# A mixture-of-experts layer on one core: the opening's loads on two queues, its first chunk in halves of the features

## The chip, the cores and the metric

One core of a Trainium2 chip runs the whole program. The metric is the device time of one execution, in microseconds; the number for the kernel before is the median of three executions.

## The reference

The input x has 128 rows of 64 tokens with 512 features (8192 tokens), and there is one condition vector of 256 numbers per row. All is float32. What is computed, in short:

```
q      = relu(cond @ W3 + b3)                       # one vector of 512 per row
h      = relu(((64 * x + sum of the row's 64 tokens) * q) @ W2 + b2)
scores = softmax(h @ gate_w.T); the 6 best of 64 experts per token
y      = for each token, its experts' SwiGLU (width 352), each weighted by its score;
         an expert takes its first 64 tokens
shared = (silu(h @ sw_gate) * (h @ sw_up)) @ sw_down      # width 704
out    = x + y + shared
```

The experts take their first 64 tokens in the order of the token numbers, so the first stage must have seen all tokens before the experts' gathers start.

## The kernel before, in words

The 8192 tokens are 16 chunks of 512 (CH). For each chunk the first stage makes h transposed (features on partitions) in four squares of 128 features; from h it makes the gate's logits, the routing, and, for every second chunk, the shared part. The second stage does the experts and the rest of the shared part. TensorE's matmuls mostly take float32r operands, a value being split into a high and a low part, three matmuls for one product (`three`, lines 1395 to 1398). The order of work on each engine is written out by hand; engines wait for each other by counting semaphores (`wait_ge`). `body(i)` does chunks 2i+1 and 2i+2.

What this case is about is the opening, up to the first `body`.

- **Loads.** SP issues nearly all: cond (line 471), W3 as one transfer of 512 KB (472), the first half of x's first chunk in four quarters (473; `load_x`, 396), W2 in four (479), the other half of the first chunk, the second chunk in four, the gate's weights (482), then the shared weights in pieces (`load_piece`). A quarter q of x or W2 goes to partitions 32q to 32q+31 only, since x is turned by VectorE in squares of 32 by 32. ACT issues the two biases, each as four loads of 128 elements one by one (`load_bias`, 724): b3 first of all, b2 behind its copy of W3.
- **q.** TensorE transposes cond (1529), ACT copies it (734), ACT and VectorE each reorder half of W3 (736, 1294), TensorE makes q with 16 matmul passes (1536), ACT takes it with bias and relu for all 128 rows into `qb` (743), each of 4 instructions for 128 features.
- **x's chain.** For each half chunk (8 blocks of 32 tokens, 128 partitions by 1024 elements) VectorE runs five operations, `x_turn`, `x_sum`, `x_pair`, `x_shift`, `x_scale` (874 to 907): the turn, the sum over each block's tokens, the sum of two blocks to a row of 64 tokens, 64 x + sum, and times q. Each waits for the one before by `x_step`.
- **W2.** ACT reorders W2 to `w2p` by columns, one copy for each block oc of 128 output features (749), each with all four blocks k of input features, then makes its high part (`split_piece(0)`).
- **First products.** `cond_half` (1417) multiplies the first chunk and the first half of the second with plain float32, two passes for a matmul (line 1429): for each half, for each oc, all four k. The second half of the second chunk goes by `three`. Then ACT takes h (`take_cond`), VectorE makes its low part (`split_h`), and `logits_raw` (1445) makes the gate's logits; for these VectorE first makes the low part of the gate's weights (1319). Which waits hold TensorE at `logits_raw(0)`: hh and hl of each square, and `gw2_ready` of both engines.
- **Fillers.** `keep_clock(n)` (1520) has TensorE transpose the identity n times into a bank that nobody reads, so that it is busy while it would wait: 6, 14 and 68 times.
- **VectorE's order** from line 1290: waits for the presets, POOL's iotas and W3; its half of W3; the first chunk's two halves; the second chunk's, mixed with the low parts of W2 and h; gate weights; rows of h (`take_rows`); `split_xm(1, 1)`, which in the kernel before also waits for `cond_begun`, since `w2p` lies where `xml1` is written.
- **POOL** makes the identity and two iotas (576 to 583) and then sleeps until the experts.

## Time and profile before

| | us |
|---|---|
| median of three executions | 1226.82 |
| lowest, highest | 1226.76, 1227.08 |
| the profiled execution, its own time | 1216.14 |
| its span, first to last instruction | 1214.4 |
| PE (TensorE matmul) busy | 1207.5 (99%) |
| PEld (weight load) busy | 893.5 (74%) |
| DVE (VectorE) busy | 856.1 (70%) |
| ACT (ScalarE) busy | 332.0 (27%) |
| POOL (GpSimd) busy | 271.0 (22%) |

A span's time is counted from the first instruction. "Busy" for PE includes matmuls that wait in its pipeline, so the spacing of weight loads (PEld) says more about its pace than the share. In the rows below, a line such as "8.78 1.25 DVE L880 ... [2.41 <-DMA x]" reads: started at 8.78, ran 1.25 us, on VectorE, line 880 of the kernel, and VectorE had been idle for 2.41 us before it, until the transfer named. SPq and ACTq are the issues of transfers on an engine's queue; their durations are those of the issue and not of the transfer. An "x4" merges four instructions, with the time from the first start to the last end.

### The profile page before, as it was taken

Reading aid. Unit: us, or ns where it says so; the run is one execution under the profiler, and the core shown is the slowest. Engines: PE = TensorE matmul, PEld = TensorE weight load, DVE = VectorE, ACT = ScalarE, POOL = GpSimd, SP = SyncE. Lnnn points to the kernel's source line nnn. Section 1 sums busy time; section 2 is a strip of 40 time slices with the busy share of each in tenths; the row PEclk is TensorE's granted clock in tenths of the full one; section 3 lists DMA queues with packets and bytes.
Section 4 is the critical chain, followed back from the end, with each engine's and each line's share of the span. In section 5 each row is a group of like instructions: output and inputs, shape, how many; then the busy total and the mean of one; then the engine's idle time right before and its main releaser. Section 6 shows DMA issues by size and latency. Waiting matters only on the chain.

```text
span 1214.4 us, 15974 instructions
## 1 busy us (share of the span) xinstructions
PE 1207.5 (99%) x5764; PEld 893.5 (74%) x5764; DVE 856.1 (70%) x1851; ACT 332.0 (27%) x630; POOL 271.0 (22%) x246
## 2 busy tenths in 40 slices
PE   9999999999999999999999999999999999999998
PEld 8888888888888888888866666666666666666666
DVE  6998989989889888886656555664655654655652
ACT  4544243433423443244111111110111201111111
POOL 0000000000000000000254356253453553543431
PEclk9999999999999999999999999999999999999999
DMA  9857445272643726246766988988979889889763
GB/s 199 212 137 194 97 118 134 83 174 64 164 106 86 183 74 157 57 134 194 248 242 232 333 278 276 346 270 273 333 249 340 291 287 295 299 290 307 275 149 86
DMA packets 159824, 250.92 MB, mean 207 GB/s; under 512 B 23617, under 2 KB 94401, under 8 KB 158593
## 3 DMA queue, kind: packets, MB, share of 16 engines
q1 hardware_dynamic: 143968, 223.66, 58.3%
q0 software_dynamic: 14048, 25.18, 10.2%
q10 hardware_dynamic: 1728, 1.05, 0.3%
q8 instruction: 46, 0.75, 0.3%
q14 instruction: 34, 0.27, 0.1%
HBM read 197.14 MB, written 61.10 MB: 213 GB/s over the span
## 4 chain that ended last, share of the span: by engine, by line
PE 94%; DVE 4%; issue 1%; ACT 0%; DMA 0%; SPq 0%; ACTq 0%
PE bank L1396 23%; PE bank L1397 22%; PE bank L1398 22%; PE bank L1598 12%; PE bank L1613 7%; PE bank L1429 2%; PE bank L1516 1%; PE bank L1517 1%; PE bank L1454 1%; PE bank L1452 1%; PE bank L1523 1%; PE bank L1465 1%; DVE x L880 0%; DVE prod L947 0%; DMA w3s<-in_L_cond_W_dram 0%
## 5 line engine op out<-in xcount | busy, mean ns | idle before, releaser
L1396 PE MATMUL bank<-hh,gu 128*128 128x512 f32 x704 | 278.0, 395 | 0.0
L1397 PE MATMUL bank<-hl,gu 128*128 128x512 f32 x704 | 274.2, 390 | 0.0
L1398 PE MATMUL bank<-hh,gu 128*128 128x512 f32 x704 | 274.0, 389 | 0.0
L591 POOL DMA_INDIRECT hg<-table,idx_quarter x128 | 125.2, 978 | 635.5 <-DVE idx_hi L1282 596.8
L1396 PEld LDWEIGHTS bank<-hh,gu 128*128 128x128 f32 x704 | 132.1, 188 | 39.1 <-issue 12.8
L1398 PEld LDWEIGHTS bank<-hh,gu 128*128 128x128 f32 x704 | 132.1, 188 | 27.9
L1397 PEld LDWEIGHTS bank<-hl,gu 128*128 128x128 f32 x704 | 132.2, 188 | 26.2
L651 ACT ACTIVATE ah<-prod 128x512 fp32r<-128x512 f32 x96 | 60.6, 632 | 302.3 <-DVE prod L947 302.3
L1355 DVE STREAM_TRANSPOSE eactT<-eact 32x96 f32<-32x96 f32 (+1 forms) x512 | 133.9, 261 | 7.9
L1396 PE MATMUL bank<-sdh,ah 128*128 128x512 f32 x320 | 125.9, 393 | 0.0
L1397 PE MATMUL bank<-sdl,ah 128*128 128x512 f32 x320 | 124.6, 389 | 0.0
L1398 PE MATMUL bank<-sdh,al 128*128 128x512 f32 x320 | 124.5, 389 | 0.0
L708 ACT ACTIVATE prod<-bank 128x512 f32<-128x512 f32 x96 | 57.1, 595 | 190.7 <-PE bank L1398 190.7
L947 DVE TENSOR_TENSOR prod<-bank,prod 128x512 f32<-128x512 f32 x96 | 65.6, 684 | 46.0 <-PE bank L1398 35.6
L1396 PE MATMUL bank<-xmh,w2h 128*128 128x512 f32 (+1 forms) x240 | 92.4, 385 | 0.0
L1398 PE MATMUL bank<-xmh,w2l 128*128 128x512 f32 (+1 forms) x240 | 91.8, 383 | 0.0
L1397 PE MATMUL bank<-xml,w2h 128*128 128x512 f32 (+1 forms) x240 | 91.7, 382 | 0.0
L1613 PE MATMUL bank<-wd,eactT 128*64 128x512 f32 (+1 forms) x384 | 89.5, 601 | 0.0
L1369 DVE TENSOR_SCALAR ysc<-bank,hsc 64x512 f32<-64x512 f32 x64 | 48.0, 750 | 56.7 <-PE bank L1613 52.6
L1343 DVE TENSOR_TENSOR eact<-bank,esilu 128x352 f32<-128x352 f32 x32 | 16.8, 525 | 99.9 <-PE bank L1598 99.9
L606 POOL DMA_INDIRECT out_dram<-ysc,idx_pair x32 | 47.8, 1494 | 157.9 <-DMA out_dram<-outst 96.8
L1598 PE MATMUL bank<-wg,hgt 128*64 128x352 f32 x512 | 81.2, 459 | 0.0
(125 smaller groups left out, 1709.9 us busy)
## 6 DMA issues: line engine op xcount, KB each, us to landing
wg<-in_L_ffn_w_gate_dram SPq DMA_DIRECT2D x64, 704.0 KB, 9.2
wu<-in_L_ffn_w_up_dram SPq DMA_DIRECT2D x64, 704.0 KB, 10.8
wd<-in_L_ffn_w_down_dram SPq DMA_DIRECT2D x64, 512.0 KB, 5.1
table<-hrow SPq DMA_DIRECT2D x64, 256.0 KB, 4.3
x<-in_x_dram SPq DMA_DIRECT2D x60, 256.0 KB, 7.0
wd<-in_L_ffn_w_down_dram SPq DMA_DIRECT2D x64, 192.0 KB, 6.1
out_dram<-outst SPq DMA_DIRECT2D x36, 256.0 KB, 4.6
outst<-in_x_dram SPq DMA_DIRECT2D x32, 256.0 KB, 3.4
```

Source lines behind the costliest of these rows:

```text
L591: nc.gpsimd.indirect_dma_start(out=hg[p % 3][:, b, :], out_offset=None, in_=quarters, in_offset=bass.IndirectOffsetOnAxis(ap=idx_quarter[: ...
L606: nc.gpsimd.indirect_dma_start(out=of, out_offset=bass.IndirectOffsetOnAxis(ap=idx, axis=0), in_=ysc[p % 3][e * CAP:(e + 1) * CAP, :], in_ ...
L651: return nc.scalar.activation(o, i, ACT.Copy)
L708: nc.scalar.activation(prod[0:m, i % 2, :], bank[t % 3][0:m, :], ACT.Silu).then_inc(s.silu_ready, 1)
L947: nc.vector.tensor_tensor(prod[0:m, i % 2, :], bank[t % 3][up0:up0 + m, :], prod[0:m, i % 2, :], ALU.mult).then_inc(s.prod_ready, 1)
L1355: op = nc.vector.transpose(eactT[feats, 0:n, tok], squares[:, 0:n, feats])
L1369: op = nc.vector.tensor_scalar(ysc[p % 3][rows, :], bank[6][rows, :], hsc[p % 3][rows, at:at + 1], None, ALU.mult)
L1396: nc.tensor.matmul(o, st_h, mv_h, start=first_mm, stop=False)
L1397: nc.tensor.matmul(o, st_h, mv_l, start=False, stop=False)
L1398: return nc.tensor.matmul(o, st_l, mv_h, start=False, stop=last_mm)
L1598: op = nc.tensor.matmul(o[half, 0:I], hgt[:, k, half], w[p % 2][e][:, k * I:(k + 1) * I], start=(k == 0), stop=(k == KC - 1))
L1613: op = nc.tensor.matmul(bank[6][half, :], eactT[0:m, it, half], wd[e][0:m, it, :], start=(it == 0), stop=(it == IT - 1))
```

## The change

Four things change, all ahead of the first `body`.

1. **Loads on two queues.** Quarters 0 and 1 (partitions 0 to 63) of x's first two chunks and of W2 stay on SP, quarters 2 and 3 (partitions 64 to 127) go to ACT's queue, between ACT's own work. W3 is one half on each. W2 comes in two steps, first the blocks k = 0, 1 of input features, then k = 2, 3.
2. **Biases as rows.** POOL loads both biases as rows of 32 elements into a cleared tile `brow`; VectorE turns it in four squares into `bcol`, where they are columns. `bias_ready` replaces the two bias waits of ACT. POOL does it ahead of its iotas, for which VectorE waits.
3. **q in two steps.** TensorE signals after each pair of 128-feature blocks; ACT takes at first only the rows that the first two chunks need (16 of 128), and the rest behind W2's copies.
4. **First chunk in halves of the features.** `x_begin` does one turn, and then sum, pair sum, shift and scale for features 0, 1 (of the four blocks k) and 2, 3 apart; `cond_first` multiplies k = 0, 1 for all four oc as soon as these are there (`x_early`), then k = 2, 3. W2 is reordered by k and not by oc. The fillers are 8, 5 and 12 in place of 6, 14 and 68.

`w2p` now lies in `xml`'s place, so `cond_begun` is gone, and SP waits for the first raw logits before it loads the fourth chunk.

```diff
@@ places and helpers
-        w2p = Place(xml1_at)("w2p", [P, KC, D])
+        w2p = Place(xml_at)("w2p", [P, KC, D])
+        bt = Place(eactT_at)
+        brow = bt("brow", [SQ, P])
+        bcol = bt("bcol", [P, SQ])
+        b3c, b2c = bcol[:, 0:KC], bcol[:, KC:2 * KC]
+        def q_of(fc):
+            return bank[3 + fc // 2][:, fc % 2 * B:(fc % 2 + 1) * B]
+        PAIRS = (slice(0, KC // 2), slice(KC // 2, KC))
+        def w2_rows(q, pair):
+            return rows_of(W2, q)[:, PAIRS[pair], :], w2s[q * SQ:(q + 1) * SQ, PAIRS[pair], :]
+        def x_quarter(n, q, half=None):
...
@@ SP
+                if n == 3:
+                    sp.wait_ge(s.lraw_filled, 1)
...
             sp.dma_start(conds[:, :], cond).then_inc(s.cond_loaded, 16)
-            sp.dma_start(w3s[:, :, :], W3.rearrange("(k p) o -> p k o", p=P)).then_inc(s.w3_loaded, 16)
-            load_x(0, 0)
+            sp.dma_start(w3s[:, 0, :], W3[0:P, :]).then_inc(s.w3_loaded, 16)
+            begin_x(0)
+            begin_w2(0)
+            begin_w2(1)
+            begin_x(1)
+            for q in range(2):
+                src, dst = x_quarter(1, q)
+                sp.dma_start(dst, src).then_inc(x_loaded[1], 16)
...
-            load_piece(0)
-            load_x(0, 1)
-            load_x(1)
@@ POOL
+            pool.wait_ge(s.bias_cleared, 1)
+            for r, b in enumerate((b3, b2)):
+                pool.dma_start(brow[r * KC:(r + 1) * KC, :].rearrange("k (q j) -> k q j", j=SQ),
+                               b.rearrange("(q k j) -> k q j", k=KC, j=SQ)).then_inc(s.bias_loaded, 16)
@@ ACT
-            load_bias(b3, b3c)
+            act.dma_start(w3s[:, 1, :], W3[P:2 * P, :]).then_inc(s.w3_loaded, 16)
...
+            begin_x(0)
             act.wait_ge(s.presets, 1)
             silu_table()
             act.wait_ge(s.condT_filled, 1)
             copy(condT[:, :, :], bank[5][:, 0:QC * B].rearrange("p (k b) -> p k b", k=QC)).then_inc(s.condT_ready, 1)
-            act.wait_ge(s.w3_loaded, 16)
+            begin_w2(0)
+            begin_w2(1)
+            act.wait_ge(s.w3_loaded, 32)
             copy(w3p[:, 1, :]...).then_inc(s.w3_ready, 1)
-            load_bias(b2, b2c)
...
+            act.wait_ge(s.bias_ready, 1)
+            for pair in range(2):
+                act.wait_ge(s.q_filled, pair + 1)
+                for fc in range(2 * pair, 2 * pair + 2):
+                    op = take_q(fc, 0, 2 * CH // N)
+                op.then_inc(s.q_ready, 1)
+            begin_x(1)
+            for q in range(2, P // SQ):
+                src, dst = x_quarter(1, q)
+                act.dma_start(dst, src).then_inc(x_loaded[1], 16)
+            def order_w2(k):
+                copy(w2p[:, k, :].rearrange("p (o a j) -> p o a j", o=KC, j=SQ),
+                     w2s[:, k, :].rearrange("p (a o j) -> p o a j", o=KC, j=SQ)).then_inc(s.w2_ready, 1)
+            act.wait_ge(s.w2_begun, 16 * (P // SQ))
+            order_w2(0)
+            order_w2(1)
+            act.wait_ge(piece_loaded[0], 16 * len(pieces[0][0]))
+            order_w2(2)
+            order_w2(3)
+            split_piece(0)
+            for fc in range(KC):
+                op = take_q(fc, 2 * CH // N, B)
             op.then_inc(s.q_ready, 1)
...
@@ VectorE
+            def x_begin(half):
...
+                x_turn(0, half)
+                total(0, 1)
+                both_halves(0, 2)
+                shift(0, 3)
+                total(1, 1)
+                scale(0, 4)
+                both_halves(1, 5)
+                shift(1, 6)
+                scale(1, 7)
...
-                    dve.wait_ge(s.cond_begun, 1)
...
+            nc.vector.memset(brow[:, :], 0.0).then_inc(s.bias_cleared, 1)
...
-            x_half(0, 0)
-            x_turn(0, 1)
-            x_sum(0, 1)
-            x_pair(0, 1)
-            x_shift(0, 1)
-            x_scale(0, 1)
+            dve.wait_ge(s.bias_loaded, 32)
+            for q in range(P // SQ):
+                part = slice(q * SQ, (q + 1) * SQ)
+                op = nc.vector.transpose(bcol[part, :], brow[:, part])
+            op.then_inc(s.bias_ready, 1)
+            x_begin(0)
+            x_begin(1)
@@ TensorE
+            def full(n, oc, half, k):
+                t = slice(half * (CH // 2), (half + 1) * (CH // 2))
+                return nc.tensor.matmul(cond_bank(n, oc)[:, t], w2p[:, k, oc * P:(oc + 1) * P], half_of(n, half)[:, :, k, :],
+                                        start=(k == 0), stop=(k == KC - 1))
+            def cond_first(half):
+                pe.wait_ge(s.x_early, half + 1)
+                for k in range(KC // 2):
+                    pe.wait_ge(s.w2_ready, k + 1)
+                    for oc in range(KC):
+                        full(0, oc, half, k)
+                pe.wait_ge(s.xm_ready, half + 1)
+                pe.wait_ge(s.w2_ready, KC)
+                for oc in range(KC):
+                    for k in range(KC // 2, KC):
+                        op = full(0, oc, half, k)
+                    if half == 1:
+                        op.then_inc(s.cond_filled, 1)
...
-            keep_clock(6)
+            keep_clock(8)
...
-            keep_clock(14)
+            keep_clock(5)
...
-            op.then_inc(s.q_filled, 1)
-            keep_clock(68)
-            for half in range(2):
-                for oc in range(KC):
-                    cond_half(0, oc, half)
+                if fc % 2 == 1:
+                    op.then_inc(s.q_filled, 1)
+            keep_clock(12)
+            cond_first(0)
+            cond_first(1)
```

## Rows read from the trace of the kernel before

**Rows 1.** Waits of PEld over the whole span: total us, times, longest.
```profile
PEld bank L1598 <- issue: 85.9, 510, 0.3
...
PEld bank L1516 <- DVE ah L865: 1.9, 1, 1.9
...
PEld bank L1454 <- DVE hl L865: 1.1, 2, 0.6
```
**Rows 2.** Chain of waits, 0 to 80 us: start, duration, what.
```profile
6.62 2.02 PE bank L1536 x16
8.64 7.42 PE bank L1523 x68
16.07 13.81 PE bank L1429 x64
```
**Rows 3.** Timeline of the opening, VectorE: start, duration, instruction, idle before it.
```profile
8.78 1.25 DVE L880 STREAM_TRANSPOSE x<-x 128x1024 f32<-128x1024 f32 x1 [2.41 <-DMA x<-in_x_dram]
...
15.90 1.25 DVE L880 STREAM_TRANSPOSE x<-x 128x1024 f32<-128x1024 f32 x1 [1.88 <-DMA x<-in_x_dram]
...
19.91 1.22 DVE L906 TENSOR_TENSOR x<-x,qb 128x1024 f32<-128x1024 f32 x1
...
21.80 1.25 DVE L880 STREAM_TRANSPOSE x<-x 128x1024 f32<-128x1024 f32 x1 [0.66 <-DMA x<-in_x_dram]
...
36.40 0.42 DVE L865 TENSOR_TENSOR gw<-bank,gw 128x256 fp32r<-128x256 f32 x1
```
**Rows 4.** Timeline, TensorE: the first matmul of the raw logits.
```profile
37.02 0.58 PE L1452 MATMUL bank<-hh,gw 128*128 128x512 f32 x1
```
**Rows 5.** Timeline from 43 to 96 us, weight loads and VectorE.
```profile
47.14 0.19 PEld L1454 LDWEIGHTS bank<-hl,gw 128*128 128x128 f32 x1 [0.54 <-DVE hl L865]
...
49.25 3.04 DVE L865 TENSOR_TENSOR gu<-gu_in,gu 128x1024 fp32r<-128x1024 f32 x3 [0.69 <-ACT gu L651]
...
94.29 0.68 DVE L865 TENSOR_TENSOR hl<-h,hh 128x512 fp32r<-128x512 f32 x1
...
95.03 0.19 PEld L1454 LDWEIGHTS bank<-hl,gw 128*128 128x128 f32 x1 [0.59 <-DVE hl L865]
```
**Rows 6.** Groups by line and shape, VectorE: busy us, mean ns; one by min/median/max ns.
```profile
L897 DVE SCALAR_TENSOR_TENSOR x<-x,vsum 128x1024 f32<-128x1024 f32 x4 | 4.9, 1223 | 0.1
...
L865 DVE TENSOR_TENSOR hl<-h,hh 128x512 fp32r<-128x512 f32 x4 | 2.7, 684 | 0.0
...
L1355 DVE STREAM_TRANSPOSE eactT<-eact x512: 237/268/274, 614.0 to 1183.2; 32x96 f32<-32x96 f32 x128, 32x64 f32<-32x64 f32 x43
```
**Rows 7.** Windows of the opening: busy PE, PEld, DVE, ACT, POOL, clock, DMA share, GB/s.
```profile
2.00:3.00 1.00, 1.00 (x6) 0.67 (x4) 0.00 (x0) 0.32 (x1) 0.00 (x0) 1.00 0.66 144
3.00:5.00 2.00, 1.98 (x10) 1.91 (x10) 0.00 (x0) 1.44 (x3) 0.00 (x0) 1.00 0.98 315
5.00:7.00 2.00, 1.75 (x12) 1.54 (x11) 0.43 (x1) 0.63 (x1) 0.00 (x0) 1.00 1.20 234
9.00:20.00 11.00, 11.00 (x84) 10.52 (x83) 8.85 (x10) 6.22 (x12) 0.00 (x0) 1.00 1.20 209
```
**Rows 8.** Window of a wide load (sw_down, 128 partitions).
```profile
51.00:52.00 1.00, 1.00 (x6) 0.84 (x5) 1.00 (x2) 0.45 (x1) 0.00 (x0) 1.00 1.15 347
```
**Rows 9.** Timeline of the opening: issues of ACT, fillers, smallest memset, copies of ACT.
```profile
0.75 1.90 ACTq L727 DMA_DIRECT2D b3c<-in_L_cond_b_dram  x4
...
1.54 0.07 DVE L1289 MEMSET zx<- 128x8 f32 x1
...
3.58 2.79 PE L1523 MATMUL bank<-ident 128*128 128x128 f32 x14
...
5.84 0.63 ACT L651 ACTIVATE w3p<-w3s 128x512 f32<-128x512 f32 x1 [1.40 <-DMA w3s<-in_L_cond_W_dram]
...
13.22 2.19 ACT L651 ACTIVATE w2p<-w2s 128x512 f32<-128x512 f32 x4 [2.26 <-DMA w2s<-in_L_cond_W_dram]
```
**Rows 10.** POOL's transfers: one in the timeline, and their us from issue to landing.
```profile
601.33 0.95 POOL L591 DMA_INDIRECT hg<-table,idx_quarter  x1 [0.30 <-issue]
...
DMA to landing us min/median/max: 2.4/5.5/8.1
```

More of the change, by code:

```diff
@@ L269, in adaln_moe_ffn_kernel @@
         piece_loaded = [sem(f"piece_loaded{n}") for n in range(1 + GT // 2 + 1 + 2)]
-        bias_loaded = [sem(f"bias_loaded{n}") for n in range(2)]
         x_begun = [sem(f"x_begun{h}") for h in range(2)]
@@ L293, in rows_of @@
             return w[q * P:(q + 1) * P, :].rearrange("(k j) i -> j k i", j=SQ)
-        pieces = [([(rows_of(W2, q), w2s[q * SQ:(q + 1) * SQ, :, :]) for q in range(P // SQ)],
+        def q_of(fc):
[4 more added lines that the diff above has]
+        def x_quarter(n, q, half=None):
+            b = slice(0, NB) if half is None else slice(half * (NB // 2), (half + 1) * (NB // 2))
+            rows = xf[n * CH + b.start * SQ:n * CH + b.stop * SQ, :].rearrange("(b i) d -> i b d", i=SQ)
+            return rows[:, :, q * P:(q + 1) * P], x32[q * SQ:(q + 1) * SQ, n % 2, b, :]
+        pieces = [([w2_rows(q, 1) for q in range(P // SQ)],
                    [(w2h[:, :, oc * P:(oc + 1) * P].rearrange("p k (a j) -> p k a j", j=SQ),
@@ L722, in split_piece, with begin_x, begin_w2 @@
                     copy(h_part, src).then_inc(s.piece_split_h, 1)
-            def load_bias(b, c):
-                with nc.allow_non_contiguous_dma(reason="a vector of 512 elements, once"):
-                    for q in range(P // SQ):
-                        act.dma_start(c[q * SQ:(q + 1) * SQ, :],
-                                      b[q * P:(q + 1) * P].rearrange("(k j) -> j k", j=SQ)).then_inc(bias_loaded[c is b2c], 16)
-            load_bias(b3, b3c)
+            act.dma_start(w3s[:, 1, :], W3[P:2 * P, :]).then_inc(s.w3_loaded, 16)
+            def begin_x(half):
+                for q in range(2, P // SQ):
+                    src, dst = x_quarter(0, q, half)
+                    act.dma_start(dst, src).then_inc(x_begun[half], 16)
+            def begin_w2(pair):
+                for q in range(2, P // SQ):
+                    src, dst = w2_rows(q, pair)
+                    act.dma_start(dst, src).then_inc(piece_loaded[0] if pair else s.w2_begun, 16)
+            begin_x(0)
             act.wait_ge(s.presets, 1)
@@ new lines, in _ @@
+            begin_x(1)
+            for q in range(2, P // SQ):
+                src, dst = x_quarter(1, q)
[7 more added lines that the diff above has]
+            act.wait_ge(piece_loaded[0], 16 * len(pieces[0][0]))
@@ L875, in x_turn @@
                 if n == 0:
-                    dve.wait_ge(x_begun[half], 64)
+                    dve.wait_ge(x_begun[half], 16 * (P // SQ))
                 elif half == 0:
@@ L1422, in cond_half @@
                     wait(pe, s.cond_taken, oc - 1)
-                if n == 0 or half == 0:
-                    pe.wait_ge(s.w2_ready, oc + 1)
+                if half == 0:
+                    pe.wait_ge(s.q_ready, 3)
                     pe.wait_ge(s.xm_ready, 2 * n + half + 1)
-                    x = half_of(n, half)
                     for k in range(KC):
-                        op = nc.tensor.matmul(cond_bank(n, oc)[:, t], w2p[:, k, oc * P:(oc + 1) * P], x[:, :, k, :],
-                                              start=(k == 0), stop=(k == KC - 1))
+                        op = full(n, oc, half, k)
                 else:
@@ L1441, in cond_half @@
                     op.then_inc(s.cond_filled, 1)
-                elif n == 1 and oc == KC - 1:
-                    op.then_inc(s.cond_begun, 1)
             def logits_raw(n):
@@ L1535, in _ @@
                 for k in range(QC):
[L1536 removed]
+                    op = nc.tensor.matmul(q_of(fc), w3p[:, k, fc * P:(fc + 1) * P],
                                           condT[:, k, :], start=(k == 0), stop=(k == QC - 1))
[L1538 to L1542 removed]
+                if fc % 2 == 1:
[3 more added lines that the diff above has]
+            cond_first(1)
             pe.wait_ge(s.gate_ready, 1)
```

90 lines of the change are left out of this document (61 added, 29 removed).

## The prediction

> **What bounds the kernel now.** I read the list of waits first. Over the whole span the longest waits of TensorE's weight loads for another engine are 1.9 and 1.1 us; the rest is "issue" between back-to-back matmuls [rows 1]. So TensorE is the bound, and the time falls only by what lets its dense work start earlier. The chain of waits shows where it is not dense: the load of W3, 16 matmuls of q, then 68 filler transposes (7.42 us) that compute nothing, and only at 16.07 the first useful product [rows 2]. The fillers stand for a wait, and VectorE's timeline says for what: its first transpose of x begins at 8.78, when x has landed; the half chunk takes it 5.23 us, to 14.01, and TensorE can't multiply before that.
>
> The reader is to see next that the first product is not what decides. VectorE works without a hole from 21.80, when the second chunk lands, to 36.82, the end of the gate's low part (36.40 plus 0.42) [rows 3]. The matmul that needs it, the first of the gate's raw logits, starts at 37.02 [rows 4]. So from 21.80 on TensorE follows VectorE with 0.2 us between them. After that everything hangs together: TensorE waits 0.54 us for hl at 47.14, VectorE 0.69 us for a piece at 49.25 and is then dense until the hl of 94.29, for which TensorE waits 0.59 us at 95.03 [rows 5]. No such wait comes later. Whatever 37.02 moves by, 95.03 and the end move by too: the links between are waits, not transfers (SP's issues up to there only come earlier). I call this move G: how much earlier VectorE ends its gate part, if TensorE can follow.
>
> **The change, part by part.**
>
> *VectorE's work.* One half chunk is now 5.23 us (15.90 to 21.13) [rows 3]. x_begin cuts sum, pair-add, shift and scale into halves of the features: nine instructions for five. A 512-element operation took 0.68 against 1.22 for 1024 [rows 6]; a dependent one starts 0.03 behind the end before, an independent one 0.1 ahead of it. Starts: turn 0, sum 1.28, pair 2.0, shift 2.2, second sum 2.8, scale 3.4, pair 4.0, shift 4.2, scale 4.9, next turn 5.55. The first pair of squares is out at 4.1, all at 5.6. From start to next start that is 5.55 against 5.13, so the cut costs VectorE 0.8 us in all (0.4 if the small ones overlap better, 1.2 if each waits). The 15.02 us behind (21.80 to 36.82) are unchanged.
>
> *Transfers.* x's first half, W3 and cond are 1.18 MB. They moved at 144 GB/s from 2 to 3, at 315 to 5 and 234 to 7, and had landed by 8.78, some 1.5 us behind their last bytes. From 9 to 20, where each transfer fills 32 partitions, the rate is 209 [rows 7]; wide transfers reach 347 on the same engines later [rows 8]. So the narrow shape, not the engines, limits. Now SP issues partitions 0 to 63 and ACT 64 to 127, both at once. No row has two such streams; the bounds are 209 and 347. I take 310, near the 315 of 3 to 5, where x's quarters began beside the wide W3. Then 1.18 MB need one microsecond at 288 and 2.9 at 310: 5.9, landed at 7.4.
>
> The Trainium skill speaks against this. "DMA: Bandwidth & Descriptors", section "Rules for kernel authors", says that spreading transfers over queues saves issue time only, and that two transfers to disjoint partition halves serialize. "SBUF — State Buffer", section "Door 1: The DMA port swizzle", says that partitions 0 to 63 reach only 8 of 16 ports (about 218 GB/s) and 64 to 127 the other 8, by which the split used here is the one that could double the rate; 209 in rows 7 agrees with its figure for 8 ports. By the first rule G is that of rival 2.
>
> *Biases.* Eight tiny loads leave ACT's queue (1.90 us to issue four [rows 9]); two go to POOL, behind one memset of VectorE (0.07). POOL's DMA instructions took 0.95 with 0.30 between them and landed 2.4 to 8.1 after issue [rows 10]: issued at 1.5 and 2.75, they land between 5.2 and 10.9; I take 6.3, nearer the first, since these carry 2 KB each. The iotas behind them end near 4.4, ahead of W3. VectorE copies w3p (0.43) and turns four 32x32 squares, each between 0.07 (its smallest memset [rows 9]) and 0.27 (32x96 [rows 6]), say 1.0 in all. So VectorE starts on x at 7.5: x allows 7.4, the biases 7.3.
>
> *ACT, TensorE's clock and q.* condT stays bound by TensorE's transposes (copied at 4.1). Then come four issues of W2 at 0.47, to 6.1, in front of w3p's copy (0.63 [rows 9]): q's 16 matmuls start at 6.9, not 6.62. The fillers' pace shows the clock: 14 in 2.79 us, 0.20 each (the 1.2 GHz level) up to 6.4, and 68 in 7.42, 0.11 each (2.4 GHz), behind q [rows 2, 9]. Now only 8, 2 and 5 precede a pause from 4.6 to 6.9, so the clock may rise later. q takes 2.0 if it is high, 16 x 0.21 = 3.4 if low; I take 3.0, low at first and rising within q: 9.9. With takes of 0.25 each (32 columns: between 0.07, the smallest operation, and the 0.63 of a copy of 512) q is ready at 10.5, in time for the first scale at 10.9. But four x issues stand behind it on ACT (to 12.4), and in front of w2p's copies (2.19 for four [rows 9]): 12.9, 13.5, 14.0, 14.6. ACT has few transfers in flight, so I expect no stall like SP's 3.06 us. The second half's ACT quarters, issued 10.5 to 11.4, land about 2.5 later, at 13.9; VectorE is free at 13.05 and waits 0.85. The second chunk lands by 18, ahead of need.
>
> *TensorE's product.* It starts at 13.0 (w2p; the early squares are there at 11.6) and takes 13.81 for 64 matmuls [rows 2]; the second half's early squares are out at 13.9 + 4.1 = 18.0, ahead of need at 19.9. It ends at 26.8 against 29.88; gate transposes 0.39, second chunk's first half 7.1: 34.3. The waits for the rest of q (ACT, near 20) and for gate_ready are hidden by the product. Moving w2p to xml's place and dropping the wait for cond_begun cost nothing: xml is first written past 62. SP's new wait for the raw logits ends 1 us after its old one, with some 15 us before that load is issued.
>
> *Sum.* VectorE starts the second chunk at 13.9 + 5.55 = 19.45 in place of 21.80: **G = 2.35**. Its gate part ends at 34.5, the logits start at 34.65, TensorE is ready at 34.3. The 3.1 us that the product gains are thus cut by VectorE.
>
> The profiled execution took 1216.14 with a span of 1214.4, so 1.7 lies around the span; the median of the runs is 1226.82, 10.7 more. G lies inside the span and is taken from the median: 1226.82 - 2.4 = 1224.4.
>
> **Rivals.**
> 1. *The clock is high by the start of q.* For it: fillers run from 1.54 to 4.6. Against: the pause. q ends at 8.9, ACT's steps come 1.0 to 1.2 earlier, x's second half no longer waits: VectorE 7.5 + 5.55 + 5.55 = 18.6, G = 3.2, TensorE ready at 33.3 and the logits at 33.8: 1223.6.
> 2. *No more bandwidth from two queues.* x at 8.2 (the first microsecond is fuller), the second half's 2.75 MB near 15.6 as at 15.90 now: VectorE 15.6 + 5.55 = 21.15, G = 0.65: 1226.2. For it: nothing in the rows shows two streams that add up; against: that wide ones reach 347 on the same engines.
> 3. *The pause behind q costs the clock.* 12 fillers end near 11.3, the product starts at 13.0. If the clock falls for as long as it took to rise (1.54 to about 6), TensorE loses up to 2 us of product and G is 0.4 to 1.2: 1226.0.
> 4. *Slower: the biases come late.* VectorE's whole chain stands behind bias_loaded. It decides from a landing at 6.5 on and loses a us per us once past x's; slower than before from 9.7 on (start 10.7, second chunk at 21.8). At the worst row, 10.9, the second chunk starts at 23.0: G = -1.2, 1228.0; a first use of POOL's queue may cost more.
> 5. *Nothing*: the fillers are only shorter, and other waits take the gain: 1226.8.
>
> **How the numbers follow.** Forecast 0.37, rival 1 0.21, rival 2 0.22, rival 3 0.06, rival 4 0.07, rival 5 0.07. A measurement of this kernel can tell about 0.2%, 2.45 us, from no change. The forecast sits on that line and gives half its 0.37 to faster, rival 1 nearly all: 0.38. Slower by more needs biases past 12: 0.04. The rest, 0.58, lies within. Predicted 1224.4. The range goes from 1222.9 (rival 1 with a cut that costs VectorE less; TensorE caps it at 3.7) to 1226.9 (rivals 2 and 5). The forecast's own range is 1223.7 to 1225.2.
>
> **What would show it.** x's first turn at 7.5 (6.8 to 8.2); a rate near 310 from 4 to 9; 64-column scales at 0.68; q's matmuls 0.21 apart, then 0.11; the first product near 13, the second chunk's turn near 19.5; a short wait in front of the raw logits; the waits near 45 and 92.7 unchanged in size. Wrong if the first turn starts after 8.5, if VectorE idles over 1.5 us before the second half, or if the waits at 47 and 95 grow by what the opening gained.

## The result: 2.7 us slower, and the profile after

The changed kernel takes 1229.44 us (median of 15 runs), the kernel before 1226.73 beside it (15 runs): ratio 1.0023, 95% interval 1.0016 to 1.0030. The forecast was 1224.4 with a range to 1226.9; the time is above the range.

The profiled execution of the changed kernel took 1228.05 with a span of 1226.3, 12 more than the profiled one of before (1216.14). These two can't be subtracted: in all 15 timed runs before took 1224.85 or more, so the profiled execution is not like them. A kernel that differs from before in one filler (again_67 below) has the same opening, and a stand of nearly all engines from about 611 to 623 us that the profiled before lacks. The openings are compared by their marks.

VectorE's timeline after (start, duration, instruction, idle before it), against [rows 3]:

```profile
8.38 0.85 DVE L1412 STREAM_TRANSPOSE bcol<-brow 32x32 f32<-32x32 f32 x4 [2.33 <-DMA brow<-in_L_cond_b_dram]
9.26 1.25 DVE L943 STREAM_TRANSPOSE x<-x 128x1024 f32<-128x1024 f32 x1
...
12.68 0.68 DVE L1011 TENSOR_TENSOR x<-x,qb 128x512 f32<-128x512 f32 x1
...
18.41 1.25 DVE L943 STREAM_TRANSPOSE x<-x 128x1024 f32<-128x1024 f32 x1 [3.52 <-DMA x<-in_x_dram]
...
23.96 1.24 DVE L943 STREAM_TRANSPOSE x<-x 128x1024 f32<-128x1024 f32 x1
...
38.56 0.42 DVE L928 TENSOR_TENSOR gw<-bank,gw 128x256 fp32r<-128x256 f32 x1
```

The line to look at is the wait of 3.52 us at 18.41: x's second half lands 2.5 later than before (15.90), and the second chunk's turn follows at 23.96 for 21.80. From there the way to the gate part is 14.60 in both (23.96 to 38.56, 21.80 to 36.40). TensorE's timeline, against [rows 2, 4]:

```profile
7.19 2.02 PE L1665 MATMUL bank<-condT,w3p 128*128 128x128 f32 x16 [1.57 <-ACT w3p L688]
9.05 1.47 PE L1652 MATMUL bank<-ident 128*128 128x128 f32 x12
13.41 7.17 PE L1534 MATMUL bank<-x,w2p 128*128 128x256 f32 x32 [2.88 <-DVE x L1011]
22.56 7.17 PE L1534 MATMUL bank<-x,w2p 128*128 128x256 f32 x32 [1.98 <-DVE x L1011]
...
39.08 0.47 PE L1581 MATMUL bank<-hh,gw 128*128 128x512 f32 x1 [1.85 <-issue]
```

The product does start 2.5 earlier (13.41 for 15.90), but its second half waits for x, and the raw logits start 2.06 later (39.08 for 37.02). They follow VectorE's gate part, which ends at 38.98. That shift stays. The wait for hl that was at 95.03 [rows 5] is now at

```profile
96.97 0.19 PEld L1583 LDWEIGHTS bank<-hl,gw 128*128 128x128 f32 x1 [0.61 <-DVE hl L928]
```

of the same size and 1.94 later, and the first expert's product starts at 610.32 for 608.37. The chain of waits (start, duration, what) names what VectorE stood for:

```profile
2.70 5.66 DMA brow<-in_L_cond_b_dram
...
9.62 8.76 DMA x<-in_x_dram
...
18.41 1.26 DVE x L943
...
37.23 1.85 issue
39.08 0.47 PE bank L1581
```

One quarter of x (128 KB), issued by ScalarE at 9.62, took 8.76 us. The DMA issues of ScalarE and of SP around it (same columns as the timelines) show in which company:

```profile
9.27 0.32 ACTq L766 DMA_DIRECT2D x<-in_x_dram  x1
9.62 0.47 ACTq L766 DMA_DIRECT2D x<-in_x_dram  x1
```

```profile
4.53 0.93 SPq L431 DMA_DIRECT2D x<-in_x_dram  x2
5.50 0.98 SPq L509 DMA_DIRECT2D x<-in_x_dram  x2
6.53 0.57 SPq L515 DMA_DIRECT2D gws<-in_L_ffn_gate_w_dram  x1
7.14 3.48 SPq L513 DMA_DIRECT2D gu_in<-in_L_ffn_sw_gate_dram  x4
```

SP had issued its own two quarters of the same half at 4.5, and behind them half of the second chunk and the gate's weights, and was at the first pieces of the shared weights, before ScalarE issued at 9.27. In the trace's packets ScalarE's queue (q10) ends with its quarters of W2 at 12.8 and starts on these quarters of x only near 14.9, over 5 us after they were issued; in between SP's queue (q1) moves its part of the second chunk alone. From 13 to 14 the view of the queues has one line (packets, MB, share of the 16 DMA engines):

```profile
q1 hardware_dynamic: 414, 0.23, 125.1%
```

So ScalarE's queue had nothing in front of these quarters and stood all the same.

### The profile page after: what moved, and what is told of

Read it like the earlier page. It is cut to its first block, busy times and chain, and to the rows that moved or that the text cites. A ratio compares the mean times of both kernels' runs of the same rounds, so it can differ in the third digit from the quotient of the medians.

```text
span 1226.3 us, 15892 instructions
## 1 busy us (share of the span) xinstructions
PE 1203.5 (98%) x5701; PEld 886.9 (72%) x5701; DVE 857.5 (70%) x1864; ACT 332.0 (27%) x634; POOL 271.6 (22%) x248
## 4 chain that ended last, share of the span: by engine, by line
PE 92%; DVE 4%; issue 1%; DMA 1%; ACT 0%; POOL 0%; POOLq 0%; ACTq 0%; DVEq 0%
PE bank L1510 22%; PE bank L1512 22%; PE bank L1511 22%; PE bank L1727 12%; PE bank L1742 7%; PE bank L1645 1%; PE bank L1646 1%; PE bank L1534 1%; PE bank L1583 1%; PE bank L1581 1%; DMA x<-in_x_dram 1%; PE bank L1594 0%; DVE x L943 0%; DMA brow<-in_L_cond_b_dram 0%; DVE prod L1059 0%
## 5 line engine op out<-in xcount | busy, mean ns | idle before, releaser
L1510 PEld LDWEIGHTS bank<-hh,gu 128*128 128x128 f32 x704 | 132.5, 188 | 41.8 <-issue 15.5
```

The source lines that it names most:

```text
L1510: nc.tensor.matmul(o, st_h, mv_h, start=first_mm, stop=False)
```

## The experiments

Ratios below are to the kernel before, timed beside each run; they can differ a little from the quotient of the medians. The theory (A): transfers start in the order in which they are issued, across both queues. The backlog is some 5 us deep, so ScalarE's late issue puts x's second half behind everything that SP has issued meanwhile. Rivals: B, ScalarE's queue is slow by itself, whatever is ahead; C, the biases' late landing (8.36) costs it. Whether two queues move more than one (rival 2 of the prediction), and what the cut costs, are questions of their own.

**x_early**: the changed kernel with ScalarE's x issues ahead of w3p's copy.
```
             begin_w2(1)
+            begin_x(1)
+            for q in range(2, P // SQ): ... x_quarter(1, q) ...
             act.wait_ge(s.w3_loaded, 32)
...
-            begin_x(1)
-            for q in range(2, P // SQ): ... x_quarter(1, q) ...
```
The lines taken out stood behind q.


> The changed kernel, with ACT issuing its quarters of x's second half and of the second chunk right behind W2's (before q is taken) and not behind q. Theory A (transfers start in the order in which they were issued, across both queues, so what was issued at 9.3 to 9.6 stood behind SP's second chunk, gate weights and first shared weights): the second half lands near 14.5 in place of 18.4, VectorE's idle 3.5 us ahead of it goes, the second chunk's turn starts at 20.4 in place of 23.96 and the first matmul of the raw logits at 35.5 in place of 39.08; about 3.6 us faster than the changed kernel, 1.5 faster than the kernel before. q is later (w3p's copy stands behind four more issues, q at 9.0) and still hidden. Theory B (a slow second ring: ACT's queue is served at a low rate whatever is ahead): landing only as much earlier as the issue, near 15.5 to 16, logits at 36.7. Theory C (the late biases are what cost it): nothing moves, logits at 39.


Measured: 1225.26 (ratio to before 0.9995, 0.9986 to 1.0004). Turns at 9.01, 15.37, 20.92; raw logits 36.04, 3.0 earlier than in the changed kernel. The landing near 15.4 lies between what A (14.5) and B (15.5 to 16) expected, so this run rules out C and doesn't tell A from B. Against the kernel before the time shows no gain clear of noise.

**hold_sp**: ScalarE as in the change; SP holds what stands behind x.
```
             begin_x(1)
+            sp.wait_ge(s.q_ready, 2)
             for q in range(2): ... x_quarter(1, q) ...
```


> The changed kernel, with one added wait: SP issues nothing behind its own quarters of x's second half until q is ready (near 9.8). ACT's issues are untouched. Theory A (issue order across queues): with only W2 ahead, ACT's quarters issued at 9.3 to 9.6 land near 15.3 in place of 18.4, raw logits at 36.0 in place of 39.08. Theory B (ACT's ring is slow by itself, 8 us from issue to landing): no change, logits at 39. Theory C (biases): no change either.


Measured: 1224.78 (0.9988, 0.9978 to 0.9997). This is the run that tells the theories apart: ScalarE issues x even later than in the change, and it lands in half the time.
```profile
10.85 0.32 ACTq L767 DMA_DIRECT2D x<-in_x_dram  x1
...
11.20 0.47 ACTq L767 DMA_DIRECT2D x<-in_x_dram  x1
```
```profile
8.74 1.25 DVE L944 STREAM_TRANSPOSE x<-x 128x1024 f32<-128x1024 f32 x1
...
15.30 1.25 DVE L944 STREAM_TRANSPOSE x<-x 128x1024 f32<-128x1024 f32 x1 [0.92 <-DMA x<-in_x_dram]
...
20.85 1.24 DVE L944 STREAM_TRANSPOSE x<-x 128x1024 f32<-128x1024 f32 x1
```
Issued at 11.20 it has landed by 15.30, 4.1 later for 8.8, and the raw logits start at 35.96: landing and logits are those that A had put on record (15.3 and 36.0). In the code only SP's issues differ, so B and C fall as the main cause.

**both**: x_early with the biases turned behind VectorE's first turn and sum (a function turn_bias, called in x_begin after the first total).


> As x_early, and VectorE turns the biases behind the first turn and sum of x and not ahead of them, so that x's chain no longer starts behind them. Theory A: the first turn starts at 7.7 in place of 9.26, the first half is done at 14.1, but the second half's landing near 14.5 then sets the pace; raw logits at 35.2, only 0.3 before x_early. Theory C (the biases are the main cost): raw logits 1.6 us before x_early, or 37.4 if x_early moved nothing.


Measured: 1225.31 (0.9988, 0.9979 to 0.9997). The first turn came at 7.39 for 9.01, so the biases did hold it. Of these 1.6 us little is left: VectorE turns the biases (0.84) inside the chain now, waits 0.32 for q and 0.71 for x, and the second turn came at 15.00 for 15.37. The raw logits, expected at 35.2, came at 36.32, later than in x_early. There they follow TensorE and not VectorE, whose gate part ended at 35.57: q started only at 9.21, the product at 15.19, and TensorE has no wait from then on.

**fewer_fillers** and **again_67**: the kernel before with 48 and with 67 filler transposes for 68.


> The kernel before with one number changed: 48 filler transposes in place of 68 ahead of the first product. The prediction's claim (from the second chunk on VectorE sets the pace, not the first product): the product starts near 14.1 in place of 15.9, TensorE gets a wait of about 1.7 us in front of the raw logits, these start at 37.0 as before, and the time is the same. The rival (TensorE's start decides): logits at 35.2 and 1.8 us less.

> The kernel before with 67 short products between q and the first product instead of 68: as good as unchanged, to see how much an opening differs from one profiled execution to the next. Profile before: first turn 8.78, second 15.90, second chunk's turn 21.80, raw logits 37.02. fewer_fillers had 8.27, 15.44, 20.60, 35.71 with the same loads. Theory (landings scatter by up to 1.2): second chunk's turn anywhere in 20.5 to 21.8 and raw logits 15.2 behind it, unless TensorE's product, which starts at 15.9, holds it at 37.0. Rival (the 48 fillers themselves brought 1.3): second chunk's turn again at 21.8 and raw logits at 37.0. The time 1225 to 1227. If the gap of 10 to 12 near 617 to 628 belongs to the machine and not to the change, it is in this profile too, span about 1225.


Measured: 1225.01 (0.9996, 0.9987 to 1.0005) and 1227.17 (1.000, 0.999 to 1.001). again_67 repeats the opening of before (8.72, 15.93, 21.35, logits 36.92). fewer_fillers was a miss: 37.0 was expected and it came to 35.71, with turns at 8.27, 15.44, 20.60. Its product started at 13.65, TensorE waited 0.25 in front of the logits, and VectorE's gate part ended at 35.60, so there the logits follow VectorE. With 68 fillers they don't. In the profiled before TensorE has no wait between its product and the logits:
```profile
15.90 13.98 PE L1429 MATMUL bank<-x,w2p 128*128 128x256 f32 x64
...
30.20 7.17 PE L1429 MATMUL bank<-x,w2p 128*128 128x256 f32 x32
```
and in calm_before (below, same opening) VectorE's part is over at 36.53, 0.87 ahead of them:
```profile
36.12 0.41 DVE L870 TENSOR_TENSOR gw<-bank,gw 128x256 fp32r<-128x256 f32 x1
```
```profile
37.40 0.58 PE L1457 MATMUL bank<-hh,gw 128*128 128x512 f32 x1
```
In all six profiles of the kernel before's opening with 67 or 68 fillers the logits start 21.12 to 21.13 behind the product's start, and 0.20 to 0.87 behind VectorE: the product, held back by the fillers, sets them. Why VectorE's own landings were early in fewer_fillers (second chunk's turn 20.60, for 21.35 to 21.81 in these six) stays open. By the VectorE of these six, 0.1 to 0.8 us is what shorter fillers alone would bring (an estimate: its distance to the logits less the 0.10 at which they follow it elsewhere).

**whole_held**: hold_sp with the first chunk's chain whole.
```
-            x_begin(0)
-            x_begin(1)
+            x_half(0, 0)
+            x_half(0, 1)
...
-                pe.wait_ge(s.x_early, half + 1)
+                pe.wait_ge(s.xm_ready, half + 1)
```


> hold_sp with the first chunk's chain and product whole (full-width operations over all features, product waits for both): takes out the cut alone. Theory: VectorE saves 0.4 in the second half (5.16 for 5.56; in the first half the gain goes into the wait for the second landing, 0.9 becomes 1.3), third turn at 20.4 for 20.85; TensorE's product starts when the whole first half is scaled, 13.9 for 13.67, as the ordering of W2 by ScalarE (done 14.0) held it in hold_sp anyway: raw logits 35.7 to 36.0, time as hold_sp's 1224.8 within 0.5. Rival (the early product in halves is what brought hold_sp under the kernel before): raw logits 37, time 1226.


Measured: 1226.84 (0.9998, 0.9989 to 1.0007). The product starts 1.1 later (14.79 for 13.67), the second chunk's turn is at 20.58 for 20.85, the raw logits at 36.01 for 35.96. The two effects cancel: without the cut VectorE is 0.3 earlier (its gate part ends at 35.59), and the later product holds the logits. So the cut is worth nothing at the raw logits here. The time was expected within 0.5 of hold_sp's 1224.8 and came 2.0 above it, on another chip, where before took 1227.07 for 1226.38; I can't say what the rest is.

**mid**: nothing of x issued late.
```
 SP:      begin_w2(0)
+         begin_x(1)
          begin_w2(1)
-         begin_x(1)
-         for q in range(2): ... x_quarter(1, q) ...
+         for q in range(P // SQ): ... x_quarter(1, q) ...
 ScalarE: begin_w2(0)
-         begin_w2(1)
+         begin_x(1)
          (copy of w3p)
+         begin_w2(1)
...
-         begin_x(1) and x_quarter(1, 2), (1, 3) behind q
```


> The change with x's second half issued between W2's two pairs on both queues, ahead of W2's second pair, W2's second pair on ScalarE behind its w3p copy, and all four quarters of the second chunk on SP: nothing of x is issued late. By theory A (transfers start in the order of issue across both queues) 0.5 MB fewer stand ahead of the second half: it lands 2.1 earlier than in hold_sp, near 13.2; VectorE has no idle behind its first turn (8.7): second turn 14.3, second chunk's turn 19.9, gate 34.6, raw logits 35.0; ScalarE, free of issues behind q, orders W2 from 11.4 and the product starts at 12.9; time 1223.9. Rival (issue order is not what counts, only the bytes in all): second half lands at 15.3 as in hold_sp, raw logits 36.0, time 1224.8.


VectorE has no wait for x behind its first turn:
```profile
9.02 1.25 DVE L940 STREAM_TRANSPOSE x<-x 128x1024 f32<-128x1024 f32 x1
14.57 1.24 DVE L940 STREAM_TRANSPOSE x<-x 128x1024 f32<-128x1024 f32 x1
20.11 1.24 DVE L940 STREAM_TRANSPOSE x<-x 128x1024 f32<-128x1024 f32 x1
```
Raw logits at 35.23, where 35.0 was expected and 36.0 by the rival: theory A again. The time, 1226.79 (0.9993, 0.9984 to 1.0002), was a miss (1223.9 expected): of 1.7 us at the raw logits and 2.0 at the first expert (606.48), both against again_67, the medians show 0.3; the interval just reaches 2.0.

**Where mid's gain went.** In again_67, a kernel before in all but one filler, the engines other than GpSimd stand or crawl: VectorE and ScalarE do next to nothing from 611 to 623, SP issues the next gate weights at 622.86 where the profiled before issues them at 611.00, and TensorE crawls from 616. Here are TensorE, VectorE, SP and GpSimd (the last gather of a row of 19 without a pause since 598.5; "remote" is a wait for which the trace names no releaser on this core):
```profile
608.52 2.59 PE L1598 MATMUL bank<-wg,hgt 128*64 128x352 f32 x16 [0.19 <-issue]
...
622.84 0.58 PE L1398 MATMUL bank<-hh,gu 128*128 128x512 f32 x1 [1.52 <-issue]
...
634.85 2.80 PE L1613 MATMUL bank<-wd,eactT 128*64 128x512 f32 x12
```
```profile
625.88 0.53 DVE L1343 TENSOR_TENSOR eact<-bank,esilu 128x352 f32<-128x352 f32 x1 [15.39 <-remote]
```
```profile
622.86 0.82 SPq L456 DMA_DIRECT2D wg<-in_L_ffn_w_gate_dram  x2
```
```profile
621.62 0.94 POOL L591 DMA_INDIRECT hg<-table,idx_quarter  x1 [0.30 <-issue]
```
From the first expert's product to its down product it takes 26.3 us; in the profiled execution of before it was 16.0 (608.37 to 624.36). In mid it took 28.2 and ended at 634.69: started 2.0 earlier, over at the same moment. The row of gathers alone doesn't do it, for the profiled before has the very same row and no stand:
```profile
598.59 1.15 POOL L591 DMA_INDIRECT hg<-table,idx_quarter  x1 [596.77 <-DVE idx_hi L1282]
...
621.47 0.94 POOL L591 DMA_INDIRECT hg<-table,idx_quarter  x1 [0.30 <-issue]
```
Theory S, for the chips on which there is a stand: a row of gathers on GpSimd that runs on past some 13 us makes the others stand, and the stand ends with the row or soon after (SP issues 0.3 after the last gather in again_67, 3.4 after it in mid).

**calm_before**: the kernel before, third and fourth pair's gathers held to the first scatter.


> The kernel before with GpSimd gathering only two pairs of experts ahead of the first (8 row gathers and 2 score gathers), the third pair's and the fourth's rows held until the first pair's scatter. In again_67 and in every profile of the changed kernels, but not in the one of before, all engines but GpSimd stand or crawl from about 611 to 623 (SP issues the next gate weights at 622.9, 11.9 after they are free), which ends with GpSimd's row of 23 gathers (621.6 + 0.9). Theory S (the engines stand for as long as GpSimd issues gathers one behind another): the gathers end at about 611.5, the gap between the first expert's products and the first down product falls from 26.3 to 16, as in the profile of before (608.4 to 624.4), span 1215 and time 1216. Rival (the gap is not tied to the gathers): gap of 26, time 1226. Second rival: the third pair's rows now come late and the engines wait there, time 1220 to 1230 with a wait of DVE on hg.


The row in again_67 is of 19 gathers, not of 23 as stated there. Measured: 1219.83 (0.9937, 0.9915 to 0.9960), where 1216 was expected; gap 16.0, and a smaller stand at 649 to 653, where the held gathers now made a new row.

**spread_before, spread_after, spread_mid, spread_mid_bias**: two pairs ahead instead of three, in four openings.


> The kernel before with GpSimd gathering two pairs ahead instead of three: rows and scores of two pairs before the first expert (10 gathers, as in calm_before), then those of pair n+2 at step n, the first of them held until the first pair's product. No row of gathers is longer than those 10. Theory S (engines stand after about 12 of uninterrupted gathers, until the row ends): neither calm_before's stall at 648 to 654 nor before's at 612 to 623 is left; expert gap 16.0, span 1214, time 1215 to 1216. Rival (calm_before's 7.8 came from the depth of the first step alone, and each next pair loses by it): 1219 or more, with waits of DVE on hg.

> The changed kernel with the same spread gathers. If the opening's loss carries through to the end without the stall, it is spread_before plus 2.0 (raw logits 39.1 for 37.0): 1217 to 1218. Rival (the later stages take it up): same as spread_before.

> mid with the same spread gathers. mid started its raw logits at 35.2 and the first expert 2.0 before the kernel before (606.5 for 608.5), but its stall lasted 1.9 longer and its time was the same. Theory (the stall hid the gain): spread_before less 1.8, 1213.5 to 1214.5, and 3.8 under spread_after. Rival (the gain is taken up elsewhere): same as spread_before within 0.5.

> spread_mid with the biases turned behind VectorE's first turn and sum. In mid VectorE's first turn starts at 9.0 behind the biases, and nothing of x is waited for after it. If the bias wait is what holds VectorE there, the first turn starts at 7.5 and the second chunk's turn 0.7 earlier (19.4), raw logits 34.9 (then TensorE, product 13.2 + 21.7, holds them), time 0.3 under spread_mid. Rival (the second half of x lands no earlier than 14.5, so the start gained is waited away, as in both): second chunk's turn 20.1, same time.


Measured: 1238.03, 1244.68, 1234.72 and 1230.14 (ratios 1.0081, 1.0105, 1.0052, 1.0032), with runs of one kernel up to 16 us apart. The times are misses: the rival held, VectorE waits for gathered rows eight times, up to 16.5 us, in spread_before. The gap was 16.0 to 16.1 as theory S has it, and three openings came as forecast: raw logits at 37.08, 35.05 and 34.72 for before, mid and mid with the late bias turn (first turn 7.76, second 14.06, third 19.61). The fourth didn't: spread_after's logits came at 40.99 for 39.1. Its q ran at the low clock (3.75), ScalarE issued x's second half at 10.98 and 11.34, and it landed 1.2 later than in the changed kernel (in held_after below, with q as slow, it landed at 18.32, so slow q alone doesn't explain that); then TensorE's clock fell behind the wait for it, and the second half of the product took 10.13 for 7.17:
```profile
23.72 10.13 PE L1536 MATMUL bank<-x,w2p 128*128 128x256 f32 x32 [2.91 <-DVE x L1013]
```

**held_before, held_after, held_mid_bias**: three pairs ahead as before, the row of gathers broken once.
```
-            for p in range(3): gather_rows / gather_scores
+            for p in range(2): gather_rows / gather_scores
...
+                    if n == 0:
+                        pool.wait_ge(s.eact_ready, 1)
+                        gather_rows(2, range(4))
+                        gather_scores(2)
                     gather_rows(n + 3, (0, 1))
```


> The kernel before with GpSimd's row of 19 gathers broken once: rows and scores of two pairs (10), then a hold until the first pair's product (about 614.9), then the third pair's and the fourth's (9), and from there all as before, three pairs ahead. Theory S (the engines stand when a row of gathers runs on past some 13): rows of 10 and 9, no stand; gap between the first expert's products and the first down product 16.0 for 26.3, nothing lost later since the depth is as before: time 1216 to 1217. Rival (the number of gathers in flight counts, not the row): the stand comes back at 622 to 632, time 1225 to 1227.

> The changed kernel with the same break. If the opening's loss goes through to the end: held_before plus 2.0 to 2.5 (raw logits 39.1 to 40 for 37.0), 1218.5 to 1219. Rival (the later stages take it up): held_before within 0.5.

> The repaired change (mid with the biases turned behind the first turn and sum; raw logits 34.7 in spread_mid_bias, 37.1 in spread_before) with the same break. If the stand had hidden the opening's gain: held_before less 2.3, 1213.7 to 1214.5, and 4.5 under held_after; against the kernel before about 12 to 13 faster. Rival (the gain is taken up elsewhere): held_before within 0.5.


Measured: 1216.26 (1.0002, 0.9993 to 1.0011), 1218.78 (1.0017, 1.0008 to 1.0026), 1213.74 (0.9979, 0.9970 to 0.9988). These ran on a chip on which the kernel before took 1216.44 (27 runs, none above 1217.7): by its time it has no stand there, so theory S was not tested, but the openings were, without a stand behind them. The change costs 2.5, the repaired change brings 2.5; at the raw logits it is 1.8 and 2.7 (38.98 and 34.52 for 37.20).

**mid_bias, held_before_2, held_mid_bias_2**: the repaired change with the row unbroken, and the last ones again, on a chip where before took 1225.87.


> The repaired change with GpSimd's gathers as in the kernel before. Where before takes 1216.4 (no stand): 2.7 under it, as held_mid_bias. Where before takes 1227 (stand): within 1 of it, since the stand then ends at the same moment in both, as in mid. Rival: 2.7 under it either way.

> held_before once more. Where before takes 1227: theory S says 1216 to 1217, and the rival (number of gathers in flight) 1225 to 1227. Where before takes 1216.4: the same as before, and nothing is told apart.

> held_mid_bias once more: 2.5 under held_before_2 in either case, 1213.7 to 1214.5 if theory S holds.


Measured: 1224.38 (0.9985, 0.9976 to 0.9994), 1216.02 (0.9916, 0.9902 to 0.9930), 1213.97 (0.9899, 0.9884 to 0.9914). Here the stand was there and the broken row took it away, as TensorE's and GpSimd's timelines of held_before_2 show:
```profile
608.15 2.59 PE L1602 MATMUL bank<-wg,hgt 128*64 128x352 f32 x16
...
624.14 2.80 PE L1617 MATMUL bank<-wd,eactT 128*64 128x512 f32 x12
```
```profile
609.87 0.94 POOL L598 DMA_INDIRECT hsc<-scores,idx_pair  x1 [0.30 <-issue]
614.52 0.95 POOL L591 DMA_INDIRECT hg<-table,idx_quarter  x1 [3.71 <-DVE eact L1347]
```
The part of theory S that can be used holds: the same gathers, 4 us of pause, 9.9 us less, and the stand doesn't come back later, as it would if the number of gathers counted. With the stand in place the repaired change shows 1.5 where within 1 was expected (gap 605.82 to 631.69, 25.9): its stand ended 3.2 before again_67's and not at the same moment as mid's did. The intervals of the two gains, 0.7 to 2.9 with the stand and 1.5 to 3.6 without, overlap. held_mid_bias_2 is the fastest version that I have, 11.9 under the kernel before on that chip. Only 2.0 of them are the opening's.

## Why the prediction was wrong, step by step

- *What bounds the kernel* held for the changed kernel and was misread for the kernel before. That TensorE follows VectorE "with 0.2 us between them" at 37.02 was taken from one profile. Six show that the product sets the logits there, fillers included, and that VectorE's nearness was chance. "The first product is not what decides" is wrong for the kernel before. It cost the forecast some 0.1 us, as VectorE stood right behind, and it hid that the fillers alone were too long. In the changed kernel, and wherever else TensorE waits in front of the logits, they start 0.10 to 0.11 behind VectorE.
- *The shift goes through*, as predicted: 2.06 at the raw logits, 1.94 at the wait near 95, 1.95 at the first expert. In all 20 profiles the first expert starts 571.2 to 571.6 behind the raw logits. In the time it was 2.5 without the stand (held_after against held_before).
- *VectorE's work* held: 5.55 from turn to turn (18.41 to 23.96).
- *x's first half* held: forecast 7.4, landed near 7.6 (the later of SP's quarters was issued at 2.1 and took 5.5). The lag of 1.5 us that went into 7.4 is 2.0 by the same rows, where 1.18 MB had moved by 6.7 and VectorE began at 8.78; that alone would have given 7.9. Its first turn with the biases out of the way was at 7.39 to 7.78.
- *The rate* did not hold in the changed kernel, where the second half's landing hangs on it. 310 GB/s was taken; from 8 to 14 it was 238, for 209 before [rows 7]. Much of that stretch had no two streams of x: ScalarE's queue moved W2, then nothing. Where both queues moved quarters of x, as in x_early from 13 to 15, it was 293, and with SP alone on the same quarters, in mid from 15 to 17, 215. The three, in this order:
```profile
8.00:14.00 6.00, 3.12 (x26) 2.83 (x26) 5.41 (x12) 2.63 (x8) 0.00 (x0) 1.00 1.15 238
```
```profile
13.00:15.00 2.00, 2.00 (x17) 1.86 (x16) 1.57 (x4) 1.90 (x5) 0.00 (x0) 1.00 1.20 293
```
```profile
15.00:17.00 2.00, 2.00 (x11) 1.76 (x10) 1.90 (x4) 1.74 (x4) 0.00 (x0) 1.00 1.23 215
```
So rival 2's premise, no more bandwidth from two queues, is wrong for two streams of x; the late issue also kept the queues from working on x side by side. (With ScalarE's quarters of x beside SP's shared weights, in the changed kernel from 15 to 18, it was 226.) The Trainium skill ("DMA: Bandwidth & Descriptors", "Rules for kernel authors") has two transfers to disjoint partition halves serialize; 293 for 215 doesn't agree with that, and it is far from the doubling that "SBUF — State Buffer", "Door 1: The DMA port swizzle", would allow two halves of 64 partitions on ports of their own.
- *Biases*: landed 8.36, not 6.3. Rival 4 was right in kind (it decides from 6.5 on), but the late turn moved the second chunk's turn by only 0.4 in both, 0.3 in spread_mid_bias (19.61 for 19.93 in spread_mid) and 0.6 in mid_bias (19.47 for 20.11 in mid). In both the wait for x takes part of it; in the other two VectorE doesn't wait for x any more, and what is lost is the turn of the biases itself, 0.84 inside the chain.
- **The step that failed** is "The second half's ACT quarters, issued 10.5 to 11.4, land about 2.5 later, at 13.9". They were issued at 9.27 and 9.62 and landed 7.8 and 8.8 later, at 17.1 and 18.4. I counted what was queued behind the instruction on its engine ("ACT has few transfers in flight") and not what the other queue had put in front of it on the same 16 DMA engines: between SP's quarters of the same half and ScalarE's, SP had issued half a chunk, the gate's weights and the first pieces. 18.41 instead of 13.9 is 4.5 us, and that turns G = +2.35 into -2.16 (23.96 for 21.80). hold_sp and x_early take that cause away and get 3.1 and 3.0 us back; mid and held_mid_bias, with x's second half in front of W2's second pair, bring the second chunk's turn to 20.11 and 19.41, for 19.45 forecast. The rate has a part in the 4.5: 4.0 MB had moved by 18.4, and at 310 GB/s they would have been through near 15 (an estimate from 253 GB/s between 2 and 3 and 310 from there). With the order set right the measured rate was enough.
- *The signs*: two of those that the prediction gave for being wrong came, a first turn after 8.5 (9.26) and VectorE idle for over 1.5 us in front of the second half (3.52).
- *q's clock*: rival 1's condition came true (q took 2.02, high clock) and brought nothing, since x's second half decided.
- *The product's start*: 13.41 for 13.0; its end and the rest followed x.
- *From the span to the time*: I took 10.7 us between the profiled and the timed executions as a constant. By again_67 it was the stand, and its length changes with the opening (gaps of 25.8 to 28.2 in the profiles that have it). Without it the loss is 2.5 and the repaired change's gain 2.5; with it they are 2.7 and 1.5 (mid_bias), and of mid's 2.0 at the first expert 0.3 are left. What sets these parts is not settled.

## What to carry to other kernels

In these runs a load moved to a second DMA queue joined the same line as the first queue's: what counted was when it was issued among both, so issue what is needed first before anything that is needed later, on either queue, and don't put it behind a wait. Ahead of every gain at the start, ask which landing is waited for next; a gain in front of it is only waited away. Fillers that stand for a wait have to be cut with the wait, and whether they or the other engine come last is read from several profiles, not from a distance of 0.2 us in one. And where the timed runs are longer than the profiled one by more than what lies around the span, take a profile that is like the timed runs before reasoning on: here 10 of the 12 us to be had were there.

## What the runs showed of the hardware

- Issue order across queues: 8.8 us from issue to landing with SP's backlog, 4.1 without, for the same 128 KB quarter; from 12.8 to 14.9 ScalarE's queue moved nothing while its quarters of x, issued by 9.62, were outstanding and SP's queue was busy.
- Two queues on the two partition halves: 293 GB/s (x_early, 13 to 15) for 215 on one queue (mid, 15 to 17), both with quarters of x.
- TensorE's clock at the start differs with equal instructions: with 8, 2 and 5 matmuls and q's start at 6.96 to 7.22, q took 2.02 in the changed kernel and spread_mid, and 3.62 to 3.75 (the 1.2 GHz level at first) in nine others, hold_sp, mid and held_after among them. With the 14 fillers of before it took 1.97 to 2.19 in all seven profiles. Where the landings stayed, it moved the raw logits by 0.2 or less (mid 35.23, spread_mid 35.05; the changed kernel 39.08, held_after 38.98). In spread_after the clock fell once more behind the wait for x: granted 0.86 of full speed from 20 to 24 and 0.52 from 24 to 30, for 1.00 in the changed kernel, and the logits came 0.85 behind VectorE.
- The stand: on three of the four chips compared before took 1224.47 or more in every run, on the fourth 1217.70 or less. In again_67, mid and the changed kernel VectorE, ScalarE and SP stop some 12 to 13 us into a row of gathers 1.25 us apart (598.5 to 611 in again_67). On a chip with the stand, rows of 10 and 9 with a pause of 4 us between them have none (held_before_2). With the same unbroken row nothing stands in the profiled before (1216.14); on which chip that ran is not on record, and what differs is not known. In the stand's course TensorE's clock falls to the lower level (mean 0.85 from 611 to 623 and 0.73 from 623 to 635 in again_67).
- What is starved is not shown. Between 608 and 624 the trace of again_67 has no packet of the queues that carry instructions, those of held_before_2 and before two each, which would fit instruction loads that wait behind the gathers. But the changed kernel has one, from 608 to 612, and stands as well. No run tried that alone.
